# A hybrid block of convolution and attention: the head norm's mean taken out of the value weights once, and values projected without padding columns

## The chip, the cores and the metric

The kernel runs on one core of a Trainium2 chip. The metric is device time in microseconds (us) from a timed execution; the kernel before took 3777.8 us (median of three runs, 3768.41 to 3781.72). The engines of the core are named as in the profile: PE (matrix products), PEld (PE's weight loads, which overlap its products), DVE (vector engine), ACT (scalar engine), POOL (GpSimd) and SP (the engine that issues the transfers here).

## The reference, cut to what matters

The network has six layers on 8 images of 32x32 positions and 128 channels. The change touches the first one only, a retention layer with 8 heads of 16 channels:

```python
vr = (xf @ Wv.T).reshape(B, L, H, HD).transpose(0, 2, 1, 3)
qk = jnp.einsum('bhqd,bhkd->bhqk', qr, kr) * mask[None]
den = jnp.clip(jnp.abs(qk).sum(-1, keepdims=True), 1.0, 50000.0)
qk = qk / den
out = jnp.einsum('bhqk,bhkd->bhqd', qk, vr).transpose(0, 2, 1, 3)
mu = out.mean(-1, keepdims=True)
var = out.var(-1, keepdims=True)
out = (out - mu) / jnp.sqrt(var + LN_EPS) * ln_g + ln_b
out = jax.nn.gelu(out.reshape(B, L, H * HD), approximate=False)
out = out @ Wo.T
```

The mean `mu` runs over the 16 channels of one head. `out` is linear in `vr`, and `vr` is linear in `Wv`, so a head's outputs have mean zero when the 16 rows of `Wv` that belong to the head have their mean subtracted. A convolution layer with an int8-like quantisation follows (the tail of an image below), then gated attention, a mixture of 16 experts, windowed attention, and a graph-routed feed-forward layer; those four are the same instructions before and after.

## The kernel before

The kernel writes out each engine's program by hand; engines meet through semaphores, and the order on each engine is the order of the code. In the retention stage an image is worked through in 32 rounds (4 passes, which are 2 groups of 4 heads times 2 halves of 512 queries, by 8 blocks of 128 keys). A round has the same core for each engine:

- PE: `score` (line 990, 4 products of 512 columns, bf16) for the next round, `norm` (line 1013, 4 f32 products with ones that sum absolute values) of the round before, whatever stands beside the rounds, and `mix` (line 1002, 4 f32 products with the values) of this round.
- DVE: the 4 products of scores with the decay table (line 2120), which free PE's banks and feed `mix`; ACT: 4 absolute values (line 1661), which feed `norm`.

Beside the rounds of image b each engine does the end of image b-1 (`tail`) and the start of image b+1 (`head`). The tuples `PROJECT_AT`, `V_AT`, `MEAN_AT`, `VAR_AT`, `WO_AT` and `CONV_AT` give the rounds in which PE has one such piece: the query and key projections (line 972), the value projections `project_v` (line 978), the head norm's means `row_mean` (line 1019), its variances `row_var` (line 1023), the output projection (line 1028) and the convolution (line 1037). DVE does the partner of such a piece one round later: `center` (line 2039) subtracts the mean that PE spread over the partitions, `rotate` (2027), `tail_add` (2044), `take_sums` (2033 and 2035). ACT squares the centred rows (`square_rows`, 1605) in rounds 7, 15, 23 and 31, takes logarithm and exponential (`invert`, 1590 to 1600) in rounds 2, 10, 18 and 26, and copies projected values out of the accumulation banks (`copy_v`, 1570). POOL divides by the sums (829) and multiplies by the inverse deviation (833).

A head has 16 channels but sits in 32 rows, since `mix` puts 4 heads into 4 strips of 32 partitions. The host lays the value weights out with 16 zero columns behind each head's 16, so `wv` has 256 columns, `project_v` gives 256 columns per block of 128 positions, and `copy_v` writes 512 columns for two blocks, zeros included. `mean_16` averages over the 16 real rows of each strip. Pieces that share bank 7 or bank 6 wait for the reader of the one before (`hn_centered`, `hn_rstd`, `qk_used` and others).

Images 0 and 1 stand apart in PE's program, images 2 to 6 are a loop, image 7 has no head, and an eighth pass of the code has only a tail. The DVE, ACT and POOL programs have a loop over images 1 to 6.

Of the kernel before, what the change touches and what calls it, by code (L numbers as in the profile page):

```python
# [24 lines left out]
P = 128  # L25
# [90 lines left out]
def build(nc, t_in, out_fm):  # L116
    ctx = ExitStack()
    with ctx:
# [83 lines left out]
        wv = sb("wv", [P, HEADS * ROWS])  # L202
# [60 lines left out]
        hn_mean = sem("hn_mean")  # L263
        hn_centered = sem("hn_centered")
# [19 lines left out]
        MEAN_AT, VAR_AT, WO_AT = (13, 21, 29, 5), (17, 25, 1, 9), (7, 15)  # L284
# [519 lines left out]
        def _(pool):  # L804
# [8 lines left out]
            for n, step in enumerate((place_step, pool_step)):  # L813
                pool.memset(pool_spare[:, 2 * n:2 * n + 1], 0.0).then_inc(step, 1)
            pool.memset(zeros16[:], 0.0).then_inc(zero_ready, 2)
# [145 lines left out]
        def _(pe):  # L961
# [13 lines left out]
            def project_v(m, n):  # L975
                for s in range(2):
                    blk = 2 * n + s
                    last = pe.matmul(banks[:, 6 + V_AT[n] % 2, s * 256:(s + 1) * 256], x_head[:, blk * P:(blk + 1) * P], wv[:],
                                     start=True, stop=True)
                last.then_inc(v_proj, 1)  # L980
# [36 lines left out]
            def row_mean(m, p):  # L1017
                pe.wait_ge(o_ready, m * PASSES + (p + 1))
                pe.matmul(banks[:, 7, :], mean_16[:], o_sb[:, p, :], start=True, stop=True).then_inc(hn_mean, 1)

# [20 lines left out]
            def beside(b, r, attend, head, tail, fresh):  # L1041
# [8 lines left out]
                if r in MEAN_AT and (tail if r == MEAN_AT[3] else attend):  # L1050
                    p = MEAN_AT.index(r)
                    if p == 0:
                        pe.wait_ge(hn_rstd, m * (2 * PASSES) + 7) if tail else pe.wait_ge(qk_used, n * 8 + 1)
                    if p == 1:
                        pe.wait_ge(qk_used, n * 8 + 7) if head else pe.wait_ge(hn_rstd, b * (2 * PASSES) + 1)
                    if p == 2:
                        pe.wait_ge(x_mid, m * 2 + 1) if tail else pe.wait_ge(hn_rstd, b * (2 * PASSES) + 3)
                    if p == 3:
                        pe.wait_ge(qk_used, n * 8 + 1) if head else pe.wait_ge(hn_rstd, m * (2 * PASSES) + 5)
                    row_mean(m if p == 3 else b, p)  # L1060
                if r in VAR_AT and (tail if r in VAR_AT[2:] else attend):
                    p = VAR_AT.index(r)
                    if p == 2 and attend:
                        pe.wait_ge(v_ready, b * 4 + 3)
                    if p == 3:
                        pe.wait_ge(wo_added, m * 2 + 1)
                    if p == 0:
                        pe.wait_ge(wo_added, m * 2 + 2) if tail else pe.wait_ge(hn_centered, b * PASSES + 1)
                    if p == 1:
                        pe.wait_ge(gn_head, (n + 1) * 4 + 3) if head else pe.wait_ge(hn_centered, b * PASSES + 2)  # L1070
# [35 lines left out]
                if head and r == 23:  # L1106
                    pe.wait_ge(hn_centered, b * PASSES + 2)
# [4 lines left out]
                if head and r in V_AT[:3]:  # L1112
# [8 lines left out]
                    if i == 2:  # L1121
                        pe.wait_ge(hn_centered, b * PASSES + 3)
# [26 lines left out]
            pe.wait_ge(qk_used, 8)  # L1149
            project_v(0, 0)  # L1150
# [10 lines left out]
            pe.wait_ge(weights_in, 16 * WEIGHT_DMAS)  # L1161
            score(0, 0)
# [398 lines left out]
        def _(act):  # L1561
# [40 lines left out]
            def square_rows(m, p):  # L1602
                act.wait_ge(hn_centered, m * PASSES + (p + 1))
# [322 lines left out]
        def _(dve):  # L1926
# [110 lines left out]
            def center(m, p):  # L2037
                dve.wait_ge(hn_mean, m * PASSES + (p + 1))
# [839 lines left out]
```

## Time and profile before

| what | value |
|---|---|
| timed runs | 3777.8 us median, 3768.41 to 3781.72 |
| profiled execution, span | 3933.9 us (no other time of that execution is given) |
| PE busy over the span | 3090.6 us, 79% |
| DVE busy | 2713.6 us, 69% |
| ACT busy | 1744.7 us, 44% |
| POOL busy | 1548.0 us, 39% |
| retention stage | about the first 1183 us of the span |

The profiled execution is 156.1 us longer than the median of the timed ones. Shares over the whole span mix six layers with different limits; the change lies in the first stage, so that stage is read by itself. In a timeline row the bracket at the end is the time for which the engine had nothing to do before this row, and what ended it; a row without a bracket followed directly on the one before. A row of a window gives its borders and length, then the busy time of each engine in it with the count of instructions, the mean granted clock of PE (1.00 is 2.4 GHz, 0.50 is 1.2 GHz) and the transfers. "x2" counts instructions in the row: an f32 product is recorded as two passes.

### The profile page before, as it was taken

Reading aid. Unit: us, or ns where it says so; the run is one execution under the profiler, and the core shown is the slowest. Engines: PE = TensorE matmul, PEld = TensorE weight load, DVE = VectorE, ACT = ScalarE, POOL = GpSimd, SP = SyncE. Lnnn points to the kernel's source line nnn. Section 1 sums busy time; section 2 is a strip of 40 time slices with the busy share of each in tenths; the row PEclk is TensorE's granted clock in tenths of the full one; section 3 lists DMA queues with packets and bytes.
Section 4 is the critical chain, followed back from the end, with each engine's and each line's share of the span. In section 5 each row is a group of like instructions: output and inputs, shape, how many; then the busy total and the mean of one; then the engine's idle time right before and its main releaser. Section 6 shows DMA issues by size and latency. Waiting matters only on the chain. (4 is left out here: it accounts for less than half of the span.)

```text
span 3933.9 us, 50351 instructions
## 1 busy us (share of the span) xinstructions
PE 3090.6 (79%) x13837; PEld 1485.8 (38%) x13839; DVE 2713.6 (69%) x3835; ACT 1744.7 (44%) x3383; POOL 1548.0 (39%) x1296
## 2 busy tenths in 40 slices
PE   5999999999975763766347777785699999988838
PEld 1222222222211333655225665662255555444412
DVE  4887788778755787999796555661266666666667
ACT  2987887778864562544234444452222222100000
POOL 1121121111000555999862222204366666666500
PEclk9999999999976676999666777776899999999968
DMA  8335415524502213776300111002111111100015
GB/s 268 84 120 152 133 48 147 147 51 129 142 11 71 79 68 120 220 217 207 120 24 27 29 30 29 29 13 51 46 33 31 31 31 25 20 5 5 4 53 203
DMA packets 236635, 319.87 MB, mean 81 GB/s; under 512 B 51789, under 2 KB 172685, under 8 KB 235929
## 3 DMA queue, kind: packets, MB, share of 16 engines
q1 hardware_dynamic: 206744, 296.77, 24.7%
q0 software_dynamic: 29696, 20.97, 3.2%
q8 instruction: 67, 1.10, 0.1%
q14 instruction: 128, 1.04, 0.1%
HBM read 170.95 MB, written 146.67 MB: 81 GB/s over the span
## 5 line engine op out<-in xcount | busy, mean ns | idle before, releaser
L1483 PE MATMUL banks<-arena 128*128 128x512 f32 (+1 forms) x1920 | 741.4, 532 | 56.7 <-DVE arena L2592 50.9
L2592 DVE TENSOR_TENSOR arena<-arena,banks 128x1280 f32<-128x1280 f32 x320 | 468.0, 1486 | 314.4 <-PE banks L1483 216.1
L1483 PEld LDWEIGHTS banks<-arena 128*128 128x128 f32 x1920 | 370.4, 194 | 478.6 <-issue 414.8
L944 POOL DMA_INDIRECT arena<-src_dram,edges_now x336 | 318.3, 947 | 243.9 <-PE banks L1483 119.4
L2120 DVE TENSOR_TENSOR arena<-banks,arena 128x512 f32<-128x512 f32 x512 | 317.7, 683 | 96.1 <-PE banks L990 75.3
L944 POOL DMA_INDIRECT arena<-dst_dram,edges_now x336 | 317.8, 946 | 108.7 <-issue 108.4
L2120 DVE TENSOR_TENSOR keys<-banks,arena 128x512 f32<-128x512 f32 x512 | 317.8, 684 | 60.6 <-PE banks L990 37.7
L2358 DVE TENSOR_TENSOR keys<-keys 128x2048 f32<-128x2048 f32 x132 | 346.1, 2661 | 1.9
L898 POOL TENSOR_TENSOR arena<-arena 128x256 f32<-128x256 f32 x144 | 339.2, 2390 | 19.7 <-ACT arena L1783 19.6
L1661 ACT ACTIVATE arena<-arena 128x512 f32<-128x512 f32 x512 | 288.2, 621 | 129.8 <-DVE arena L2120 89.3
L990 PE MATMUL banks<-arena 96*128 96x512 bf16 x1024 | 281.9, 389 | 35.1 <-DVE arena L2120 32.5
L1661 ACT ACTIVATE keys<-keys 128x512 f32<-128x512 f32 x512 | 281.5, 619 | 53.3 <-PE banks L1013 45.8
L1840 ACT ACTIVATE arena<-arena,mx 128x128 f32<-128x128 f32 x256 | 99.9, 393 | 334.5 <-DVE mx L2416 328.0
L829 POOL TENSOR_TENSOR work<-work,keys 128x512 f32<-128x512 f32 x32 | 40.9, 1279 | 503.4 <-ACT keys L1597 503.4
L808 POOL TENSOR_TENSOR pool_spare<-pool_spare 128x1 f32<-128x1 f32 x54 | 17.8, 329 | 524.3 <-DVE edges_now L2557 241.7
L1303 PE MATMUL banks<-arena 128*128 128x64 bf16 x1152 | 151.3, 307 | 78.0 <-DVE arena L2403 63.7
L990 PEld LDWEIGHTS banks<-arena 96*128 96x128 bf16 x1024 | 80.7, 98 | 339.6 <-DVE arena L2120 119.4
L1886 ACT ACTIVATE arena<-banks,mb 128x512 f32<-128x512 f32 x128 | 87.8, 688 | 241.2 <-PE banks L1468 126.4
L1303 PEld LDWEIGHTS banks<-arena 128*128 128x128 bf16 x1152 | 142.8, 148 | 101.1 <-DVE arena L2403 74.0
L1474 PE MATMUL banks<-arena 128*128 128x512 f32 x256 | 138.2, 630 | 53.7 <-ACT arena L1886 37.5
L1279 PE MATMUL banks<-arena 128*128 128x128 f32 x584 | 104.5, 303 | 94.7 <-POOL arena L898 94.6
L1891 ACT ACTIVATE keys<-banks,mb 128x512 f32<-128x512 f32 x64 | 44.0, 688 | 300.3 <-PE banks L1474 224.2
(397 smaller groups left out, 5727.5 us busy)
## 6 DMA issues: line engine op xcount, KB each, us to landing
sorted_dram<-zeros SPq DMA_DIRECT2D x8, 8192.0 KB, 29.1
arena<-in_w SPq DMA_DIRECT2D x150, 384.0 KB, 4.1
arena<-parts_dram SPq DMA_DIRECT2D x192, 128.0 KB, 4.8
experts_dram<-keys SPq DMA_DIRECT2D x64, 256.0 KB
keys<-experts_dram SPq DMA_DIRECT2D x8, 2048.0 KB, 8.5
parts_dram<-nodes SPq DMA_DIRECT2D x16, 768.0 KB, 3.3
slot_out_dram<-zeros SPq DMA_DIRECT2D x8, 1280.0 KB, 32.0
arena<-sorted_dram SPq DMA_DIRECT2D x150, 64.0 KB, 3.3
```

The lines of the kernel that those rows point to most:

```text
L898: pool.tensor_tensor(slot_hid[:, j % RING], slot_silu[:, j % RING], slot_up[:, j % RING], ALU.mult)\
L944: pool.indirect_dma_start(to[:, s, t, :], None, table[:, :], bass.IndirectOffsetOnAxis(edges_now[:, s, n, t:t + 1].bitcast(U32), 0)).then_ ...
L990: pe.matmul(banks[:, j, :], k_st[0:STACK, head, a * P:(a + 1) * P], q_st[0:STACK, head, halves(qh)], start=True, stop=True).then_inc(score ...
L1279: last = pe.matmul(banks[:, 4 + j % 2, 0:C], slot_hid[:, j % RING, n * P:(n + 1) * P], staged[:, j, 2 * HIDDEN + n * C:2 * HIDDEN + (n + 1 ...
L1303: last = pe.matmul(out, count_low[:, r, :, t], count_high[:, r, :, t], start=start and t == 0, stop=stop and t == CHUNK - 1, skip_group_ch ...
L1474: pe.matmul(banks[:, 6 + i % 2, :], m2[:, e, c, :], mh[:, 2 * (i % 2) + c, :], start=(c == 0), stop=(c == CHUNKS - 1)).then_inc(m_out, 1)
L1483: last = pe.matmul(banks[:, bank, 0:part.shape[1]], ohl[:, s, t, :], part, start=False, stop=False, skip_group_check=True)
L1661: act.activation(a_slots[r % 2][:, j, :], p_slots[r % 2][:, j, :], ACT.Abs).then_inc(absolute, 1)
L1840: act.activation(sc[:, k % 2, j, :], sc[:, k % 2, j, :], ACT.Exp, bias=mx[:, k % 2, 1, j:j + 1], accum_out=mx[:, k % 2, 2, j:j + 1]).then_ ...
L2120: dve.tensor_tensor(p_slots[r % 2][:, j, :], banks[:, j, :], table[:, PER_GROUP * g + j, at:at + HALF], ALU.mult).then_inc(masked, 1)
L2358: dve.tensor_tensor(vo[:, t], vi[:, 0], vi[:, 1], ALU.max if t else ALU.min).then_inc(sort_step, 1)
L2592: dve.tensor_tensor(rh[:, t % RH], oha[:, s, t:t + 1, :].broadcast_to([P, VALS, NB]), vals[:, t, :].unsqueeze(2).broadcast_to([P, VALS, NB ...
```

## The change

The mean is subtracted from the value weights on the chip, once: three small DVE operations after the first image's normalisation (`wv_mean`, a sum over 16 columns per head, a scale, a subtraction), announced by `wv_centered`, for which PE waits before the first `project_v`. `row_mean` and `center` go, and with them 4 PE products and 4 DVE subtractions per image, 32 of each in all. `square_rows` waits for the division (`o_ready`) instead of the subtraction; the PE pieces that waited for `hn_centered` wait for another reader of their bank. `wv` has 128 columns, `project_v` gives 128 columns per block, and `copy_v` reads 256 columns and writes them in groups of 16 with gaps of 16, which POOL has cleared once (`L1["v"]`, announced by `v_cleared`). Instructions of other layers, and the transfers apart from the smaller `wv`, are as they were.

```diff
         wqk = sb("wqk", [P, 4, P])
-        wv = sb("wv", [P, HEADS * ROWS])
+        wv = sb("wv", [P, HEADS * KD])
+        wv_mean = sb("wv_mean", [P, HEADS])
...
-        MEAN_AT, VAR_AT, WO_AT = (13, 21, 29, 5), (17, 25, 1, 9), (7, 15)
+        VAR_AT, WO_AT = (17, 25, 1, 9), (7, 15)
...
+            pool.memset(L1["v"], 0.0).then_inc(v_cleared, 1)
             pool.memset(zeros16[:], 0.0).then_inc(zero_ready, 2)
...
-                    last = pe.matmul(banks[:, 6 + V_AT[n] % 2, s * 256:(s + 1) * 256], x_head[:, blk * P:(blk + 1) * P], wv[:],
+                    last = pe.matmul(banks[:, 6 + V_AT[n] % 2, s * P:(s + 1) * P], x_head[:, blk * P:(blk + 1) * P], wv[:],
...
-            def row_mean(m, p):
-                pe.wait_ge(o_ready, m * PASSES + (p + 1))
-                pe.matmul(banks[:, 7, :], mean_16[:], o_sb[:, p, :], start=True, stop=True).then_inc(hn_mean, 1)
...
-                if r in MEAN_AT and (tail if r == MEAN_AT[3] else attend):
...
-                    row_mean(m if p == 3 else b, p)
...
                     if h == 0:
-                        pe.wait_ge(hn_centered, m * PASSES + 4)
-                    elif attend:
-                        pe.wait_ge(hn_centered, b * PASSES + 1)
+                        pe.wait_ge(qk_used, n * 8 + 1) if head else pe.wait_ge(hn_rstd, m * (2 * PASSES) + 5)
...
+            pe.wait_ge(wv_centered, 1)
             project_v(0, 0)
...
+            pe.wait_ge(v_cleared, 1)
             score(0, 0)
...
-                act.activation(v_sb[:, 2 * n:2 * n + 2, :].rearrange("p k n -> p (k n)"), banks[:, 6 + V_AT[n] % 2, :], ACT.Copy)\
+                if n == 0:
+                    act.wait_ge(v_cleared, 1)
+                act.activation(v_sb[:, 2 * n:2 * n + 2, :].rearrange("p k (h e) -> p (k h) e", h=HEADS)[:, :, 0:KD],
+                               banks[:, 6 + V_AT[n] % 2, 0:2 * P].rearrange("p (k e) -> p k e", e=KD), ACT.Copy)\
                     .then_inc(v_ready, 1)
...
             def square_rows(m, p):
-                act.wait_ge(hn_centered, m * PASSES + (p + 1))
+                act.wait_ge(o_ready, m * PASSES + (p + 1))
...
-            def center(m, p):
-                dve.wait_ge(hn_mean, m * PASSES + (p + 1))
-                dve.tensor_tensor(o_sb[:, p, :], o_sb[:, p, :], banks[:, 7, :], ALU.subtract).then_inc(hn_centered, 1)
...
             head_normalise(0)
+            by_head = wv[:].rearrange("p (h e) -> p h e", h=HEADS)
+            once(dve.tensor_reduce(wv_mean[:], by_head, AX.X, ALU.add))
+            once(dve.tensor_scalar(wv_mean[:], wv_mean[:], 1.0 / KD, None, ALU.mult))
+            dve.tensor_tensor(by_head, by_head, wv_mean[:].unsqueeze(2).broadcast_to([P, HEADS, KD]), ALU.subtract)\
+                .then_inc(wv_centered, 1)
...
-    t["wv"] = head_cols(a["L0_conv_Wv"])
+    t["wv"] = a["L0_conv_Wv"].T
```

On PE in round 5 of image 1, before (990 is `score`, 1013 `norm`, 1019 the mean, 1002 `mix`, 972 a projection):

```order
L990 MATMUL banks<-arena 128x512 [waits masked] x4
L1013 MATMUL banks<-arena,ones 32x512 [waits absolute]
L1013 MATMUL banks<-arena,ones 32x512 x3
L1019 MATMUL banks<-work,mean 128x512 [waits o_ready,qk_used]
L1002 MATMUL banks<-keys,arena 32x512 [waits masked,v_ready]
L1002 MATMUL banks<-keys,arena 32x512 x3
L990 MATMUL banks<-arena 128x512 [waits masked] x4
L1013 MATMUL banks<-keys,ones 32x512 [waits absolute]
L1013 MATMUL banks<-keys,ones 32x512 x3
L972 MATMUL banks<-keys,wqk 128x512 [waits qk_used,head_normed]
```

The same place after, with lines two higher for the same functions:

```order
L992 MATMUL banks<-arena 128x512 [waits masked] x4
L1015 MATMUL banks<-arena,ones 32x512 [waits absolute]
L1015 MATMUL banks<-arena,ones 32x512 x3
L1004 MATMUL banks<-keys,arena 32x512 [waits masked,v_ready]
L1004 MATMUL banks<-keys,arena 32x512 x3
L992 MATMUL banks<-arena 128x512 [waits masked] x4
L1015 MATMUL banks<-keys,ones 32x512 [waits absolute]
L1015 MATMUL banks<-keys,ones 32x512 x3
L974 MATMUL banks<-keys,wqk 128x512 [waits qk_used,head_normed]
```

The mean product between `norm` of round 4 and `mix` of round 5 is gone, and nothing takes its place.

On PE in rounds 28 and 29 of image 1, before (978 is the value projection):

```order
L978 MATMUL banks<-wv,keys 128x256 [waits v_ready]
L978 MATMUL banks<-wv,keys 128x256
L1002 MATMUL banks<-arena 32x512 [waits masked,v_ready]
L1002 MATMUL banks<-arena 32x512 x3
L990 MATMUL banks<-arena 128x512 [waits masked] x4
L1013 MATMUL banks<-arena,ones 32x512 [waits absolute]
L1013 MATMUL banks<-arena,ones 32x512 x3
L1019 MATMUL banks<-work,mean 128x512 [waits o_ready,x_mid]
L1002 MATMUL banks<-keys,arena 32x512 [waits masked,v_ready]
L1002 MATMUL banks<-keys,arena 32x512 x3
L990 MATMUL banks<-arena 128x512 [waits masked] x4
L1013 MATMUL banks<-keys,ones 32x512 [waits absolute]
```

The same place after:

```order
L980 MATMUL banks<-wv,keys 128x128 [waits v_ready]
L980 MATMUL banks<-wv,keys 128x128
L1004 MATMUL banks<-arena 32x512 [waits masked,v_ready]
L1004 MATMUL banks<-arena 32x512 x3
L992 MATMUL banks<-arena 128x512 [waits masked] x4
L1015 MATMUL banks<-arena,ones 32x512 [waits absolute]
L1015 MATMUL banks<-arena,ones 32x512 x3
L1004 MATMUL banks<-keys,arena 32x512 [waits masked,v_ready]
L1004 MATMUL banks<-keys,arena 32x512 x3
L992 MATMUL banks<-arena 128x512 [waits masked] x4
```

The value projection keeps its two products with half the columns, and the mean of round 29 is gone.

## Rows read from the trace of the kernel before

**Rows 1.** Two images: busy (count) of PE, PEld, DVE, ACT, POOL; clock; DMA.

```profile
187.50:323.50 136.00, 127.64 (x722) 32.41 (x721) 110.30 (x188) 110.52 (x181) 24.03 (x16) 0.99 0.42 118
463.40:603.20 139.80, 132.29 (x723) 32.78 (x722) 110.39 (x189) 110.86 (x182) 23.66 (x16) 0.95 0.41 115
```

**Rows 2.** Groups by line: shapes, count, busy us, mean ns, idle before.

```profile
L1019 PE MATMUL banks<-work,mean 128*128 128x512 f32 x64 | 36.9, 660 | 5.1 <-POOL work L829 5.1
...
L2039 DVE TENSOR_TENSOR work<-work,banks 128x512 f32<-128x512 f32 x32 | 22.0, 686 | 11.6 <-PE banks L1019 11.6
...
L1570 ACT ACTIVATE arena<-banks 128x512 f32<-128x512 f32 x32 | 18.5, 579 | 2.2 <-PE banks L978 2.2
...
L1782 ACT ACTIVATE arena<-banks 128x256 f32<-128x256 f32 x144 | 55.6, 386 | 58.8 <-PE banks L1271 45.6 <-POOL arena L898 12.7
```

**Rows 3.** Timeline of PE, round 5: start, length, name, idle before.

```profile
619.79 1.13 PE L1019 MATMUL banks<-work,mean 128*128 128x512 f32 x2
620.85 1.06 PE L1002 MATMUL banks<-keys,arena 128*32 128x512 f32 x8
```

**Rows 4.** Timeline of DVE, the subtraction after that product.

```profile
620.96 0.69 DVE L2039 TENSOR_TENSOR work<-work,banks 128x512 f32<-128x512 f32 x1 [0.21 <-PE banks L1019]
622.27 2.48 DVE L2120 TENSOR_TENSOR keys<-banks,arena 128x512 f32<-128x512 f32 x4 [0.63 <-PE banks L990]
```

**Rows 5.** Timeline of PE, round 21 and the start of round 22.

```profile
546.50 1.12 PE L1019 MATMUL banks<-work,mean 128*128 128x512 f32 x2
...
550.34 0.39 PE L990 MATMUL banks<-arena 96*128 96x512 bf16 x1 [1.72 <-DVE arena L2120]
```

**Rows 6.** Timeline of DVE, after round 15 and in round 22.

```profile
523.42 0.69 DVE L2044 TENSOR_TENSOR work<-work,banks 128x512 f32<-128x512 f32 x1 [1.07 <-PE banks L1028]
...
549.60 2.48 DVE L2120 TENSOR_TENSOR arena<-banks,arena 128x512 f32<-128x512 f32 x4
```

**Rows 7.** Timeline of PE, the wait of round 12 in two images.

```profile
231.97 1.07 PE L1013 MATMUL banks<-keys,ones 128*32 128x512 f32 x8 [2.21 <-ACT keys L1661]
...
507.88 1.93 PE L1013 MATMUL banks<-keys,ones 128*32 128x512 f32 x8 [2.21 <-ACT keys L1661]
```

**Rows 8.** Timeline of PE, rounds 26 and 28 of one image.

```profile
568.90 0.39 PE L990 MATMUL banks<-arena 96*128 96x512 bf16 x1 [2.09 <-DVE arena L2120]
...
573.10 2.08 PE L978 MATMUL banks<-wv,keys 128*128 128x256 f32 x4
...
583.61 1.13 PE L978 MATMUL banks<-wv,keys 128*128 128x256 f32 x4
584.67 1.07 PE L1002 MATMUL banks<-arena 128*32 128x512 f32 x8
```

**Rows 9.** Timeline of PE, 128-column f32 products of a later stage.

```profile
1703.08 1.06 PE L1271 MATMUL banks<-arena 128*128 128x128 f32 x8
1703.97 0.27 PE L1264 MATMUL banks<-ident,arena 128*128 128x128 f32 x1
```

**Rows 10.** Timelines of DVE and of PE's weight loads, where two images meet.

```profile
597.04 2.48 DVE L2120 TENSOR_TENSOR arena<-banks,arena 128x512 f32<-128x512 f32 x4 [2.45 <-issue]
...
599.58 0.10 PEld L990 LDWEIGHTS banks<-arena 96*128 96x128 bf16 x1 [0.50 <-DVE arena L2120]
```

**Rows 11.** Timelines of ACT and PE after the last image's last round.

```profile
1146.12 0.81 ACT L1609 ACTIVATE work<-work,lngb 128x512 f32<-128x512 f32 x1 [0.78 <-POOL work L833]
...
1147.84 2.08 PE L1028 MATMUL banks<-work,wo 128*128 128x512 f32 x2 [0.78 <-DVE work L2039]
```

**Rows 12.** Timeline of ACT, round 23 of the first image.

```profile
155.36 2.19 ACT L1661 ACTIVATE keys<-keys 128x512 f32<-128x512 f32 x4 [0.39 <-PE banks L1013]
```

**Rows 13.** Timelines of DVE and POOL at the start of the program.

```profile
19.47 0.69 DVE L2027 TENSOR_TENSOR keys<-banks,arena 128x512 f32<-128x512 f32 x1 [2.17 <-PE banks L972]
...
0.94 0.53 POOL L815 MEMSET zeros<- 128x512 bf16 x1
23.16 1.26 POOL L819 TENSOR_TENSOR keys<-keys 128x512 f32<-128x512 f32 x1 [21.70 <-DVE keys L2027]
```

More of the change, by code:

```diff
@@ L262, in build @@
         sum_step = sem("sum_step")
-        hn_mean = sem("hn_mean")
-        hn_centered = sem("hn_centered")
+        wv_centered = sem("wv_centered")
+        v_cleared = sem("v_cleared")
         hn_var = sem("hn_var")
@@ L1049, in beside @@
                     project_v(b, 3)
-                if r in MEAN_AT and (tail if r == MEAN_AT[3] else attend):
[L1051 to L1059, printed above, removed]
-                    row_mean(m if p == 3 else b, p)
                 if r in VAR_AT and (tail if r in VAR_AT[2:] else attend):
                     p = VAR_AT.index(r)
-                    if p == 2 and attend:
-                        pe.wait_ge(v_ready, b * 4 + 3)
+                    if p == 2:
+                        pe.wait_ge(v_ready, b * 4 + 3) if attend else pe.wait_ge(x_mid, m * 2 - 1)
                     if p == 3:
@@ L1067, in beside @@
                     if p == 0:
-                        pe.wait_ge(wo_added, m * 2 + 2) if tail else pe.wait_ge(hn_centered, b * PASSES + 1)
+                        pe.wait_ge(wo_added, m * 2 + 2) if tail else pe.wait_ge(qk_used, n * 8 + 1)
                     if p == 1:
-                        pe.wait_ge(gn_head, (n + 1) * 4 + 3) if head else pe.wait_ge(hn_centered, b * PASSES + 2)
+                        pe.wait_ge(gn_head, (n + 1) * 4 + 3) if head else pe.wait_ge(hn_rstd, b * (2 * PASSES) + 1)
                     row_var(m if p >= 2 else b, p)
@@ L1106, in beside @@
                 if head and r == 23:
-                    pe.wait_ge(hn_centered, b * PASSES + 2)
+                    pe.wait_ge(qk_used, n * 8 + 7)
                     head_mean(n + 1)
@@ L1121, in beside @@
                     if i == 2:
-                        pe.wait_ge(hn_centered, b * PASSES + 3)
+                        pe.wait_ge(x_mid, m * 2 + 1) if tail else pe.wait_ge(hn_rstd, b * (2 * PASSES) + 3)
                     project_v(n, i)
@@ L2059, in beside @@
                     rotate(n, PROJECT_AT.index(r - 1))
-                if r - 1 in MEAN_AT:
-                    p = MEAN_AT.index(r - 1)
-                    if p == 3 and tail:
-                        center(m, 3)
-                    elif p < 3 and attend:
-                        center(b, p)
                 if tail and r - 1 in WO_AT:
@@ L2816, in lay_out @@
     t["edges"] = a["L3_ffn_edge_index"].reshape(2, P, COLS)
-    def head_cols(w):
-        full = np.zeros((C, HEADS, ROWS), w.dtype)
-        full[:, :, :KD] = w.T.reshape(C, HEADS, KD)
-        return full.reshape(C, HEADS * ROWS)
     swap = np.arange(C) ^ 1
     t["wqk"] = np.stack([a["L0_conv_Wq"].T, a["L0_conv_Wq"][swap].T, a["L0_conv_Wk"].T, a["L0_conv_Wk"][swap].T], 1)
-    t["wv"] = head_cols(a["L0_conv_Wv"])
+    t["wv"] = a["L0_conv_Wv"].T
     wo = np.zeros((HEADS, ROWS, C), np.float32)
```

## The prediction

> **What bounds the kernel now.** I read the page's slices first, then the windows of single images in the retention stage, then the timelines of PE, DVE and ACT through one image, stopping wherever PE's row has a bracket. The windows say which engine fills an image: in the steady one PE is busy for 132.3 of 139.8 us, DVE for 110.4 and ACT for 110.9 [rows 1]. So PE bounds the stage, but not all the time: 7.5 us of the image PE stands still. The timeline shows where. One wait is in round 12 (2.21 us, for ACT's absolute values) [rows 7], one in round 22 (1.72 us, for DVE's table products) [rows 5], one in round 26 (2.09 us, DVE again) [rows 8]; the rest is in short ones beside these. Everywhere else PE's rows follow each other without a bracket, and DVE has brackets that name PE [rows 4]. Whatever PE loses in such a full stretch, the image loses; what it loses ahead of one of the waits only lengthens the wait.
>
> A second thing to see is the clock. The same wait of 2.21 us is followed by 8 passes that take 1.07 us in image 1 and 1.93 us in the steady image [rows 7], which is 2.4 against 1.2 GHz; the mean granted clock is 0.99 there and 0.95 here, and the image takes 136.0 against 139.8 us [rows 1]. The work is the same, so 3.8 us of the steady image are the clock's.
>
> **The mean products.** 64 passes make 32 products [rows 2]. In a full stretch one costs from its own start to the start of what follows, 620.85 - 619.79 = 1.06 us [rows 3]; the 660 ns mean of a pass counts the overlap twice. An image has four, in rounds 5, 13, 21 and 29. Those of rounds 5, 13 and 29 stand in full stretches: 3 x 1.06 = 3.2 us per image. The one in round 21 does not. There DVE goes from 523.42, where it last waited for PE, through its statistics and the normalisation of the image before to the table product at 549.60 [rows 6], and PE, whose mean product starts at 546.50, waits 1.72 us for that [rows 5]. Without the product PE waits 2.8 us. I take nothing for it; the bound on the other side is 1.06.
>
> **The subtractions on DVE.** 32 of 0.686 us [rows 2]. Between two table products DVE waits 0.21 us for PE, subtracts for 0.69 and waits for PE another 0.63 [rows 4], 1.53 us together. Take PE's 1.06 away, and 0.47 us of waiting for PE is left: DVE stays the one that waits, which is also why the whole 1.06 is taken as gained above. None lies in DVE's chain to the waits of rounds 22 and 26. Worth 0, at most 0.7 each. The squares on ACT no longer wait for them, which matters only at the end of the stage.
>
> **The value projection.** In a full stretch a `project_v` costs 584.67 - 583.61 = 1.06 us for 4 passes of 256 columns [rows 8]. For 128 columns the nearest row is a later stage's: 8 passes begin at 1703.08 and the next product at 1703.97, so 0.11 us a pass, 0.45 for four [rows 9]. Saved: 0.6 us; the bounds are 0 (the weight loads, which stay, set the pace) and 0.7 (a third of the time left). The Trainium skill, "TensorE: Matmul & The Clock Gate", section "LDWEIGHTS (loading the stationary operand)", speaks against a full halving: a weight load takes its number of columns over 1.2, in ns, so 107 ns for 128, and here the image's block is the weight, unchanged. By that, four passes cannot take under 0.43 us as an estimate, a saving of 0.63; the trace's 0.11 us a pass agrees.
>
> Of the four in an image, that of round 0 and that of round 28 are in full stretches: 2 x 0.6. That of round 26 runs at the lower clock, 2.08 us [rows 8]; half of it is 1.0. That of round 31 is lost: DVE comes over its loop's end with 2.45 us in which it waits for nothing, and PE's next `score` is released by its table product (0.50 us) [rows 10]. So 2.2 us per image.
>
> `copy_v` goes from 579 ns towards the 386 of a 128x256 copy [rows 2], 32 times 0.2 us on ACT, in stretches where ACT waits for PE: 0. That its write has gaps no row shows; were it as slow as now, nothing changes, and at double, 0.6 us each, ACT's waits still cover it.
>
> **Images of another shape.** Image 0 has no tail and thus not the two DVE waits, but ACT is nearly the limit: in round 23 it waits just 0.39 us for PE [rows 12]. I give it 1.06 (round 13), 0.4 (round 21), 0.9 (round 29) and 0.8 for two value projections: 3.2. Images 1 to 6 get 3.2 + 2.2 = 5.4 each, 32.4. Image 7 gets three means and one projection: 3.8. In the last tail nothing lies beside the chain. `Gelu` on ACT begins at 1146.12 for 0.81 us, and PE's output projection at 1147.84, because of the mean and the subtraction [rows 11]; without them it follows the `Gelu` at 1146.97, 0.9 us sooner. At the start value projections stand once alone in a chain of PE and ACT: at the lower clock one is shorter by 1.0 and its two copies by 0.2 each, if no transfer is later; so 0 to 1.4, and I take 0.7.
>
> **What is added.** Three DVE operations on 128x128 or less fit into the 2.17 us for which DVE waits before its first rotation [rows 13]; the nearest row, 0.69 us for 512 columns, makes them 2.1 us at most. The clearing of 2048 f32 columns on POOL: 512 of bf16 took 0.53, so four to eight times that, 2 to 4 us, and POOL has nothing before 23.16 [rows 13]. Both 0. No wait is new in a loop: the pieces of PE that waited for the subtraction now wait for rotations or deviations that are rounds old.
>
> Sum: 3.2 + 32.4 + 3.8 + 0.9 + 0.7 = 41.0 us. The profiled execution's 3933.9 would become 3893; it is 156.1 us above the median of the timed runs, and since nothing shows where these lie I subtract the same 41 from 3777.8: 3737 us.
>
> **The rivals.** (1) The clock comes back. If a wait no longer drops the clock, as in image 1, each of images 2 to 6 gains up to 3.8 us more, 19 in all: 3718. For it: the same pause did not drop it in image 1. Against: images 2 to 6 are one loop, and the steady one has it. The mirror of it, a longer half-rate stretch in some places, is in the range too.
>
> (2) The round becomes bound elsewhere. If a round without its mean product is held by ACT or DVE, as in round 21 and in image 0, the products of rounds 5, 13 and 29 are worth a third or nothing and the projections remain: 7 x 2.2 + some 4, 20 us: 3758. Against: the 0.47 us for which DVE would still wait for PE in such a round [rows 4]; ACT has 29 us of idle time per image [rows 1].
>
> (3) Slower. PE's wait in round 22 grows from 1.7 to 2.8 us, and the clock stays low from there to the wait of round 26. Between these, from 550.3 to 566.8 (568.90 less its wait), PE is the bound for 16.5 us [rows 5, 8]. A mean clock of 0.95 means a tenth of the image, 14 us, at half rate [rows 1], some 5 us behind each of the three waits. If all 16.5 were at half rate the other 11.5 would take as long again: 11.5 - 5.4 = 6.1 us more per image in six images, less the 8.6 us saved in images 0 and 7 and at both ends: +28, 3806 us. It decides once the low clock costs 5.4 us more per image than now. For it: a value projection 4 us behind the wait of round 26 was still at 2.08 us [rows 8]. Against: the mean clock of 0.95 leaves no room for more than such short stretches after any of the pauses as they are [rows 1]. The same page of the Trainium skill, section "HAM oscillation — how this bites in real kernels", says that a pause of the engine can throttle it again, so that the burst behind starts cold; of the two images in [rows 7] one agrees and one does not.
>
> (4) The change does nothing measurable: the profiled execution has waits that the timed ones have not, or the other way round. 3778.
>
> **How the numbers follow.** Forecast 0.62, (1) 0.17, (2) 0.12, (3) 0.05, (4) 0.04. The time is the forecast's, 3737. The measurement tells about 0.3% from no change, 11 us. The range reaches to rival (1) and a little past, and up past (2), since the runs before spread over 13 us: 3712 to 3764. Faster by over 0.3% are the forecast, (1) and nearly all of (2): 0.90; within 0.3% 0.06; slower 0.04.
>
> **What would show it.** In the profile after: image windows of about 134.4 us in place of 139.8, PE busy about 125 us; PE's wait in round 22 at 2.8 us and those in rounds 12 and 26 as they are; value projections of four passes that take 0.45 to 0.5 us to the next start; the wait at the images' boundary longer by 0.6 on PE; the later layers as long as before. Images that stay near 139 with new brackets on PE in rounds 5 to 8 would mean rival (2), a mean granted clock above 0.97 or below 0.92 in the steady images (1) or (3).

## The result, and the profile after

The changed kernel takes 3772.3 us (median of 12 runs, 3764.0 to 3782.9) against 3781.1 us for the kernel before (12 runs, 3768.4 to 3793.4). The medians lie 8.7 us apart. The ratio on record is 0.9964, with a 95% interval of 0.9952 to 0.9976; it is not the quotient of the two medians (0.9977), and by it the gain is some 14 us. Either way the gain is measurable and small. The forecast was 3737 us, a gain of 41, in a range of 3712 to 3764.

First the windows of the retention's images, one row an image, in the order length, busy time and count of PE, PEld, DVE, ACT and POOL, granted clock, DMA share and GB/s. Here are images 1 and 2 and one of the later ones, of the changed kernel.

```profile
183.34:319.76 136.42, 127.42 (x714) 31.63 (x713) 107.77 (x185) 109.85 (x181) 23.66 (x16) 0.94 0.42 118
319.76:456.02 136.26, 123.55 (x707) 31.08 (x709) 108.01 (x184) 109.75 (x181) 23.66 (x16) 0.95 0.45 124
456.02:596.33 140.31, 127.78 (x717) 31.92 (x721) 108.03 (x183) 109.60 (x181) 23.68 (x16) 0.93 0.39 115
```

PE's busy time has fallen by 4.5 us in the later images, as was to be expected of the instructions taken out, and yet such an image takes 140.3 us where it took 139.8 [rows 1]. Image 1 takes 136.4 where it took 136.0, at a clock of 0.94 where it had 0.99. So PE stands still for longer, 12.5 us instead of 7.5, and what it does runs slower.

The timeline of PE shows two places. The first is where the loop's body ends and begins again (round 31 of one image and round 0 of the next):

```profile
726.57 0.71 PE L980 MATMUL banks<-wv,keys 128*128 128x128 f32 x4
727.21 1.06 PE L1004 MATMUL banks<-keys,arena 128*32 128x512 f32 x8
730.71 1.03 PE L992 MATMUL banks<-arena 96*128 96x512 bf16 x4 [2.43 <-issue]
731.67 1.47 PE L1015 MATMUL banks<-keys,ones 128*32 128x512 f32 x8
733.07 0.58 PE L980 MATMUL banks<-wv,keys 128*128 128x128 f32 x1
735.70 0.80 PE L980 MATMUL banks<-wv,keys 128*128 128x128 f32 x3 [2.05 <-issue]
736.43 1.94 PE L1004 MATMUL banks<-arena 128*32 128x512 f32 x8
738.30 1.38 PE L992 MATMUL banks<-arena 96*128 96x512 bf16 x4
```

Two brackets of 2.43 and 2.05 us have `issue` as their releaser: no other engine is waited for. That PE's own instructions were not there is a reading of them, which the next rows and the experiments test. Even a value projection is cut in two, one pass and then three. Behind them 8 passes take 1.94 us, the lower clock. Each of the loop's four turns back has such a pair of brackets, 17.9 us in all (10.0 on `score`, 7.9 on the projection). The kernel before has no such bracket inside its retention loop. The branch at the loop's end tells the same: duration in ns, minimum, median and maximum, of the kernel before and then of the changed one.

```profile
L1165 PEldq COMPARE_BRANCH  x5: 83/215/232, 455.9 to 1014.0; - x5
```

```profile
L1152 PEldq COMPARE_BRANCH  x5: 83/4828/5084, 444.3 to 1007.2; - x5
```

The queue that brings instructions agrees: packets, MB and share, of the whole page, before and after. From 600 to 760 us it moves 10 packets in the changed kernel; from 460 to 620 us of the kernel before it has none. Over the whole loop, from 330 to 1000 us, the queue moves 41 packets in the changed kernel and 6 in the kernel before, these 6 ahead of 460 us.

```profile
q8 instruction: 67, 1.10, 0.1%
```

```profile
q8 instruction: 84, 1.38, 0.2%
```

The second place is round 22, which answers to [rows 5]:

```profile
677.71 1.04 PE L1004 MATMUL banks<-keys,arena 128*32 128x512 f32 x8
681.66 2.40 PE L992 MATMUL banks<-arena 96*128 96x512 bf16 x4 [2.91 <-DVE arena L2100]
683.99 1.93 PE L1015 MATMUL banks<-keys,ones 128*32 128x512 f32 x8
685.86 0.37 PE L1090 MATMUL banks<-ident,small 128*1 128x128 f32 x1
686.15 1.87 PE L1004 MATMUL banks<-arena 128*32 128x512 f32 x8
```

The wait has grown from 1.72 to 2.91 us, and the products behind it run at the lower clock for longer. In the same place the kernel before had this:

```profile
552.61 1.94 PE L1013 MATMUL banks<-keys,ones 128*32 128x512 f32 x8
554.47 0.37 PE L1105 MATMUL banks<-ident,small 128*1 128x128 f32 x1
554.77 1.48 PE L1002 MATMUL banks<-arena 128*32 128x512 f32 x8
```

So the first 8 passes behind the wait were at half rate already. The change lengthens that stretch: the second 8 now take 1.87 us, and the four `score` products 2.40. A value projection in a full stretch takes 727.21 - 726.57 = 0.64 us where it took 1.06 [rows 8], more than the 0.45 to 0.5 that was forecast. In the last tail PE's output projection follows `Gelu` directly (1135.30 - 1134.34 = 0.96 us, where it was 1.72 [rows 11]). Of ACT, then of PE:

```profile
1134.34 0.81 ACT L1599 ACTIVATE work<-work,lngb 128x512 f32<-128x512 f32 x1 [0.77 <-POOL work L835]
```

```profile
1135.30 3.49 PE L1026 MATMUL banks<-work,wo 128*128 128x512 f32 x4 [7.16 <-ACT work L1599]
```

The layers behind the retention play no part. In the changed kernel's execution they take 2605 us (the span less the last convolution product's start, as in the table below), and in eleven of the experiments' twelve 2591 to 2605. In the twelfth they take 2612 us, and in the profiled execution of the kernel before 2752. The excess of 156 us of that execution thus lies in them and not in its retention: 1181.8 us, which a run with the same retention repeats (1184.7).

### The profile page after: what moved, and what is told of

Same layout as the page of the kernel before. It is cut to its first block and busy times, and to the rows that moved or that the text cites. A ratio compares the mean times of both kernels' runs of the same rounds, so it can differ in the third digit from the quotient of the medians.

```text
span 3772.9 us, 50157 instructions
## 1 busy us (share of the span) xinstructions
PE 3018.5 (80%) x13775; PEld 1464.9 (39%) x13775; DVE 2700.6 (72%) x3806; ACT 1732.5 (46%) x3383; POOL 1547.7 (41%) x1297
## 3 DMA queue, kind: packets, MB, share of 16 engines
q8 instruction: 84, 1.38, 0.2%
## 5 line engine op out<-in xcount | busy, mean ns | idle before, releaser
L1470 PE MATMUL banks<-arena 128*128 128x512 f32 (+1 forms) x1920 | 725.7, 524 | 13.3 <-DVE arena L2577 13.1
L992 PE MATMUL banks<-arena 96*128 96x512 bf16 x1024 | 291.9, 400 | 51.2 <-DVE arena L2100 38.2
L913 POOL DMA_INDIRECT arena<-slot_out_dram,arena x128 | 158.5, 1238 | 43.8 <-issue 43.6
```

Source lines behind the costliest of these rows:

```text
L913: pool.indirect_dma_start(made[:, j, :], None, slot_out_dram[:, :], bass.IndirectOffsetOnAxis(rows_now[:, j:j + 1].bitcast(U32), 0)).then_ ...
L992: pe.matmul(banks[:, j, :], k_st[0:STACK, head, a * P:(a + 1) * P], q_st[0:STACK, head, halves(qh)], start=True, stop=True).then_inc(score ...
L1470: last = pe.matmul(banks[:, bank, 0:part.shape[1]], ohl[:, s, t, :], part, start=False, stop=False, skip_group_check=True)
```

## The experiments

Two theories stood against each other and a third beside them. **Fetch:** the loop's body is shorter and stands elsewhere in PE's program, and there it no longer stays in PE's instruction memory. **Clock:** idle time that the change adds ahead of PE's half-rate stretches lowers the granted clock. **Waits:** the image is held by ACT and DVE, rival (2) of the prediction. The table holds all runs. "Retention" is the start of its last convolution product in the profiled execution; "images" are the windows of images 1 to 5, and beside them their granted clocks; ratio and interval are against the kernel before as it was timed with each. The experiments were timed in three groups: both loops placed, loop misplaced, attention loop moved and mean's part; retention loop placed, V's part, products in round 13 and in round 21; and the last four. Across groups the ratios compare better than the medians.

| kernel | median us | ratio, 95% interval | retention | images | clock in them |
|---|---|---|---|---|---|
| before | 3781 to 3787 | 1 | 1181.8 | 136.1 to 140.1 | 0.95 to 0.99 |
| after | 3772.3 | 0.9964 [0.9952, 0.9976] | 1167.6 | 136.3 to 141.5 | 0.92 to 0.95 |
| after, both loops placed | 3748.8 | 0.9899 [0.9877, 0.9920] | 1152.2 | 133.9 to 136.5 | 0.94, 0.95 |
| after, retention loop placed | 3754.4 | 0.9908 [0.9883, 0.9932] | 1150.7 | 132.0 to 136.5 | 0.94 to 0.97 |
| before, retention loop misplaced | 3839.5 | 1.0142 [1.0119, 1.0164] | 1233.0 | 138.4 to 148.7 | 0.93 to 0.96 |
| before, attention loop moved | 3789.4 | 1.0008 [0.9991, 1.0025] | 1184.7 | 137.7 to 140.0 | 0.95 to 0.98 |
| placed, mean's part alone | 3753.9 | 0.9914 [0.9897, 0.9931] | 1154.4 | 131.7 to 137.6 | 0.94 to 0.99 |
| before, V's part alone | 3765.9 | 0.9950 [0.9933, 0.9966] | 1161.1 | 134.7 to 138.5 | 0.95 to 0.99 |
| placed, product in round 13 | 3745.6 | 0.9893 [0.9869, 0.9917] | 1149.9 | 134.5 to 136.3 | 0.95, 0.96 |
| placed, product in round 21 | 3738.2 | 0.9871 [0.9848, 0.9893] | 1131.7 | 129.3 to 133.3 | 0.96 to 1.00 |
| placed, product in round 22 | 3765.4 | 0.9952 [0.9935, 0.9969] | 1158.7 | 134.8 to 136.6 | 0.94, 0.95 |
| placed, products in 21 and 11 | 3742.3 | 0.9893 [0.9872, 0.9913] | 1133.6 | 129.5 to 133.2 | 0.96 to 1.00 |
| placed, products in 21, 11, 25 | 3735.7 | 0.9860 [0.9835, 0.9884] | 1131.7 | 129.5 to 134.7 | 0.95 to 1.00 |
| before, products in 11 and 25 | 3767.4 | 0.9952 [0.9934, 0.9970] | 1160.5 | 134.4 to 136.0 | 0.99, 1.00 |

**The changed kernel with both loops placed.** The body of the retention's loop begins at PE's instruction 3009 of the compiled program before (counted without labels, 1655 long) and at 2976 in the changed one (1635 long). Waits on a semaphore that has long reached its value move it; two of them make one instruction.

```
+            for _ in range(66):                       # ahead of head_mean(0)
+                pe.wait_ge(consts_in, 16 * CONST_DMAS)
...
+            for _ in range(446):                      # behind the retention
+                pe.wait_ge(consts_in, 16 * CONST_DMAS)
```

> The changed kernel, with satisfied waits added to TensorE's program at two places where it is idle: 33 instructions ahead of the first head mean, which put the body of the retention loop back at the place (modulo 256 instructions) where it stands in the kernel before, and 223 between the retention and the windowed attention, which keep the attention's loop body where the changed kernel has it (modulo 256). Theory (instruction fetch): in the changed kernel the retention loop no longer stays in TensorE's instruction memory, so each backward branch waits for its instructions (2.4 and 2.0 us at the first two rounds, a branch of 4.8 to 5.1 us, and a low clock behind it). Here these waits go (branch 0.1 to 0.3 us, no instruction fetches inside the loop), the images of the loop fall from 140.3 to about 136 us, the stage ends some 18 us earlier (about 1150 us), and the kernel takes 3750 to 3760 us. Rival A (the images are bound by what ScalarE and VectorE hand over): the waits for instructions go but the images stay at 140 us, time as the changed kernel, 3772. Rival B (the clock falls because TensorE has less to do): images stay at 140 us at a granted clock of 0.93 or less.

3748.8 us, just under the 3750 to 3760 of the fetch theory. The branch is at 0.21 us (median), and the queue moves 6 packets from 330 to 1000 us. An image of the loop:

```profile
453.64:588.49 134.85, 125.80 (x714) 31.40 (x713) 107.81 (x185) 109.64 (x181) 23.66 (x16) 0.95 0.43 119
```

At the kernel before's clock, 0.95, it takes 134.85 us, 4.95 less than before. If ACT and DVE held the image, as the waits theory has it, it would not have become shorter.

**The kernel before with its retention loop misplaced.** The same waits, 446 ahead of `head_mean(0)` and 66 behind the retention, in the kernel before.

> The kernel before with nothing changed but its place: 223 satisfied waits ahead of the first head mean, so that the retention loop's body begins at the place (modulo 256 instructions) that it has in the changed kernel, and 33 behind the retention, so that everything after it stands as in the kernel before. Fetch theory: the retention loop now fetches its instructions in every turn; each image of the loop goes from 139.8 to 144 to 145 us, the kernel from 3781 to about 3800 us. Rivals A and B: no fetch matters, 3781 within 5.

It went the theory's way, but by 57 us instead of 20. Of that, 22.6 us are the waits themselves, which here the whole start stood behind; DVE's first normalisation begins at 39.08 us and not at 16.49.

```profile
39.08 0.81 DVE L2017 TENSOR_SCALAR keys<-keys,small 128x1024 f32<-128x1024 f32 x1
```

The retention ends 51.2 us later, less 22.6 is 28.6 us. Of these, 2.8 stand in images 0 and 1, ahead of the loop, where its fetches cannot reach; the other 26 are what a misplaced loop costs, with nothing else changed. From 330 to 1000 us the queue moves 40 packets. The branch and an image of the loop:

```profile
L1167 PEldq COMPARE_BRANCH  x5: 83/4871/5298, 479.8 to 1067.0; - x5
```

```profile
491.84:638.20 146.36, 133.72 (x725) 32.96 (x729) 110.67 (x187) 110.78 (x181) 23.67 (x16) 0.94 0.40 110
```

**The kernel before with its attention loop moved.** 358 waits between the retention and the attention, which bring the attention's loop to where the changed kernel has it.

> The kernel before with 179 satisfied waits of TensorE between the retention and the windowed attention alone, so that the attention loop's body begins where it begins in the changed kernel (modulo 256 instructions). Fetch theory: no fetches within the attention loop, its stage falls from 681 us to about 660 us as in the changed kernel, and the time from 3781 to about 3760 us, with none of the change in it. Rivals: stage and time as in the kernel before, within 5 us.

This missed. No time was gained (1.0008), although the instruction fetches within that loop did go: in its stage the queue moves 10 packets, and 28 in the kernel before. Its stage, from the first product with `wqkv` on V's side to the last transposition, takes 662 us in this run, and 649 in the run before this one, whose loop fetches throughout. The 682 us from which I had taken a gain of 20 belong to the one execution that was profiled. In this stage, where PE often waits for DVE and ACT, the fetches cost nothing that the times show.

**The change in halves.** First the mean's part with V padded as before, both loops placed as in the first run.

```
+        wv = sb("wv", [P, HEADS * ROWS])
...
+            by_head = wv[:].rearrange("p (h e) -> p h e", h=HEADS)[:, :, 0:KD]
```

> The changed kernel with V projected with its zero padding as before (the mean's part alone), with the same added waits as the first run of this call, both loops placed alike. By the prediction's terms the narrower projection is 2.2 us an image (0.6 in rounds 0 and 28, 1.0 in round 26), so this should be some 15 us slower than the first run (about 3770). If the narrower projection hides behind other work, it is as fast as the first run.

3753.9, 5 us behind the first run and not 15: nearer the second reading. Then V's part in the kernel before, its mean products kept.

```
...
-                    last = pe.matmul(banks[:, 6 + V_AT[n] % 2, s * 256:(s + 1) * 256], x_head[:, blk * P:(blk + 1) * P], wv[:],
+                    last = pe.matmul(banks[:, 6 + V_AT[n] % 2, s * P:(s + 1) * P], x_head[:, blk * P:(blk + 1) * P], wv[:],
...
```

> The kernel before with V projected without its zero padding and nothing else changed (its retention loop stands one instruction later, which the fetch theory calls harmless). The prediction's terms: 0.6 us each in rounds 0 and 28, 1.0 in round 26, 15 us in all (3766). By the run of the mean's part alone, which was only 5 us behind the run of both, 2 to 6 us (3777).

3765.9, a ratio of 0.995: 19 us, above the 15 of the terms and far above 2 to 6. Alone the parts shorten the retention by 20.7 us (V) and 27.4 us (mean), together by 31.1 (retention loop placed), not 48. An image of each tells why, the mean's part first (two images of one execution), V's second:

```profile
458.24:589.96 131.72, 122.83 (x714) 31.17 (x713) 107.81 (x185) 110.42 (x181) 23.66 (x16) 0.99 0.44 122
589.96:727.53 137.57, 128.90 (x714) 32.13 (x713) 107.80 (x185) 110.65 (x181) 23.64 (x16) 0.94 0.42 117
```

```profile
598.90:733.80 134.90, 126.22 (x722) 31.56 (x721) 110.31 (x189) 109.84 (x181) 24.04 (x16) 0.99 0.43 119
```

The same instructions take 131.7 us at a clock of 0.99 and 137.6 at 0.94. In the run of V's part the clock rises from 0.95 in image 1 to 0.99 in images 4 and 5, in that of the mean's it reaches 0.99 in one image alone. The durations add, the clock does not.

**The retention's loop placed and nothing more.** The first run without its second group of waits.

> The changed kernel with the 33 added instructions ahead of the first head mean alone; the 223 behind the retention are left out, so the attention's loop stands elsewhere. By the runs so far the place of the attention's loop is worth nothing (660 us with and without fetches), so this should be as fast as the run with both pads or a few us faster: 3742 to 3750 us. If the attention's place does matter, 3760 to 3770.

3754.4 (3744 to 3758), above the 3742 to 3750 expected and not apart from the first run. The branch is back at a fifth of a microsecond, and this is the kernel from which the next runs are built. One image at each of two clocks:

```profile
L1154 PEldq COMPARE_BRANCH  x5: 76/208/227, 449.8 to 989.1; - x5
```

```profile
457.30:593.60 136.30, 127.37 (x714) 31.66 (x713) 107.77 (x184) 109.71 (x181) 23.64 (x16) 0.94 0.42 118
593.60:725.70 132.10, 123.02 (x715) 30.80 (x713) 107.87 (x185) 109.69 (x181) 23.66 (x16) 0.97 0.43 122
```

**One mean product put back.** Its result is unused and nothing is subtracted; the retention's loop stays at 3009. In round 13 first:

```
+                if r == 13 and attend:
+                    pe.wait_ge(hn_rstd, m * (2 * PASSES) + 7) if tail else pe.wait_ge(qk_used, n * 8 + 1)
+                    pe.wait_ge(o_ready, b * PASSES + 1)
+                    pe.matmul(banks[:, 7, :], mean_16[:], o_sb[:, 0, :], start=True, stop=True)
```

> The run before this one (changed kernel, retention loop at the old place) with the averaging product of round 13 back on TensorE, its result unused and nothing subtracted. The prediction's theory: round 13 is no wait's cover, so the product costs its full 1.06 us an image, 8 us in all, and if the half-rate stretches fall on it somewhat more. Rival (the images are bound by ScalarE or VectorE): nothing. Second rival (a product that TensorE computes keeps its clock up): nothing or a gain, at a granted clock of 0.95 instead of 0.94.

It was to cost 8 us and cost nothing: 3745.6 against 3754.4, with intervals that overlap, at a clock of 0.95 and 0.96 in place of 0.94 to 0.97. So more work in a full stretch came with a slightly higher clock too; whether it raised it, one run does not tell. The same in round 21:

> The same with the averaging product of round 21 back instead, its result unused. The prediction's theory: the wait of round 22 on VectorE's table product shrinks from 2.9 to 1.8 us and the time stays, within 2 us of the kernel without it; that is what made this one of the four products free. Rival: it costs 1.06 us an image like the other, 8 us. Second rival (clock): less idle time ahead of the half-rate stretch, a gain of some us.

3738.2 against 3754.4: more work, 16 us less time, the clock theory's side (14 by the ratios). Two images, and PE's rounds 21 and 22:

```profile
187.80:317.10 129.30, 121.05 (x716) 30.79 (x715) 107.74 (x185) 109.42 (x181) 23.64 (x16) 1.00 0.43 125
448.60:581.70 133.10, 125.57 (x716) 31.46 (x715) 107.66 (x184) 109.50 (x181) 23.65 (x16) 0.96 0.42 121
```

```profile
528.87 1.13 PE L1051 MATMUL banks<-work,mean 128*128 128x512 f32 x2
529.93 1.07 PE L1004 MATMUL banks<-keys,arena 128*32 128x512 f32 x8
532.71 0.39 PE L992 MATMUL banks<-arena 96*128 96x512 bf16 x1 [1.71 <-DVE arena L2105]
...
534.82 1.07 PE L1015 MATMUL banks<-keys,ones 128*32 128x512 f32 x8
```

The wait is 1.71 us again, and the 8 passes behind it take 1.07 us, not 1.94. The windows of images 0 to 5 give the clock's share: their lengths times what is missing of the clock to 1.00 add up to 36 us with the retention loop placed and nothing more, and to 17 with the product in round 21. The difference, 19 us, accounts for all by which the retention became shorter (1150.7 to 1131.7, of which 1.1 us is an earlier start, since fewer waits are added there). The control is the same product issued one round later, behind that wait (`if r == 22 and attend:`).

> As the run with the unused product in round 21 (3738 us), but the product is issued one round later, behind the wait of round 22 instead of ahead of it. The work is the same, the idle time of round 22 is not filled. Clock theory (idle time of TensorE ahead of the stretches from 84 and 102 us into an image is what drops the clock): the wait stays at 2.9 us, an image has 13.7 to 17.1 us at half rate as without the product, and the time is 3750 to 3760. Rival (it is the work added, not where it stands, or the product's other effects): 3738 as with the product in round 21.

```profile
535.90 1.04 PE L1004 MATMUL banks<-keys,arena 128*32 128x512 f32 x8
539.85 2.40 PE L992 MATMUL banks<-arena 96*128 96x512 bf16 x4 [2.91 <-DVE arena L2105]
542.18 1.94 PE L1015 MATMUL banks<-keys,ones 128*32 128x512 f32 x8
544.05 2.08 PE L1051 MATMUL banks<-work,mean 128*128 128x512 f32 x2
```

3765.4: 27 us slower by the medians and 31 by the ratios than with the product ahead of the wait, at the same count of instructions and the same loop position. Where the product stands decides. Behind the wait it fills no idle time and runs at half rate itself, 2.08 us in seven of the eight images and 1.06 in the first, 16 us in all; this run is 11 us slower than the one without any product by the medians, and 17 by the ratios (0.9952 against 0.9908).

**Filling the other waits.** An unused product in round 11, ahead of the wait of round 12, and then one in round 25 as well, ahead of the wait of round 26:

```
+                if r == 11 and head and attend:
+                    pe.wait_ge(qk_used, n * 8 + 4)
+                    pe.matmul(banks[:, 6, :], wqk[:, 0, :], x_head[:, halves(0)], start=True, stop=True)
+                if r == 25 and head and attend:
+                    pe.wait_ge(gn_head, (n + 1) * 4 + 3)
+                    pe.matmul(banks[:, 7, :], wqk[:, 0, :], x_head[:, halves(0)], start=True, stop=True)
```

> The kernel with the unused product in round 21 (3738 us), and one more unused product of 1.06 us in round 11, ahead of the wait of 2.2 us of round 12. Clock theory: the wait falls to 1.1 us, the half-rate stretch at 43 us into an image (3.4 us in two images of five) goes, and the time is the same or up to 5 us shorter: 3732 to 3738. Rival (a product costs its duration): 8 us longer.

> As the run before, and a third unused product in round 25, ahead of the wait of 2.1 us of round 26 (it stands ahead of the variance product of round 25, so it delays that by 1 us). Clock theory: the half-rate stretch from 100 us into an image goes as well, images of 129 to 130 us at a granted clock of 0.99 to 1.00, and 3720 to 3732 us. Rival: each product costs its 1.06 us an image, 16 us longer than with the one of round 21 alone (3754).

The one in round 11 did not pay: 3742.3 (3737 to 3751) beside 3738.2 (3725 to 3740). Its images take 129.5 to 133.2 us as without it, and its retention ends 1.9 us later; but the ratios, 0.9893 and 0.9871, are 8 us apart with overlapping intervals, so the rival's cost of 8 us is not excluded. With all three it is 3735.7, not apart from the product in round 21 alone; I had hoped for 3720 to 3732. Some images have the full clock and some do not:

```profile
317.20:446.70 129.50, 123.23 (x721) 31.33 (x719) 107.72 (x184) 109.46 (x181) 23.70 (x16) 1.00 0.45 125
446.70:581.40 134.70, 129.04 (x721) 32.12 (x719) 107.79 (x184) 109.65 (x181) 23.67 (x16) 0.95 0.42 119
```

Last, the two products in the kernel before, with nothing taken out and no other edit (its loop begins 16 instructions later and still stays):

> The kernel before with two unused products of 1.06 us added, in round 11 and in round 25, ahead of the waits of rounds 12 and 26, and nothing taken out. Clock theory: images of 139.8 us with 13.7 us at half rate become some 136 us (as image 1 of the kernel before, 136.1 with 3.4 us at half rate): 15 to 25 us faster, 3760. Rival (a product costs its duration): 16 us slower, 3800.

```profile
459.50:593.90 134.40, 128.16 (x726) 32.46 (x725) 110.31 (x188) 110.45 (x181) 24.03 (x16) 1.00 0.43 120
```

3767.4, a ratio of 0.9952: two useless products bring the kernel before as much as the whole change did when it was made. Here too the clock accounts for it: what is missing of it to 1.00, times the lengths of images 0 to 5, falls from 29 to 8 us, and the retention is 21.3 us shorter.

## Why the prediction was wrong, point by point

**The terms of the sum held in all, not one by one.** Image 0 was to gain 3.2 us and gained 3.1 (115.8 to 112.7); a steady image 5.4, and at an equal clock of 0.95, with the loop in its place, the loop's three images at that clock, in two runs, gained 4.95 to 5.5; the last tail 0.9, measured 0.8. A value projection was to gain 0.6 in a full stretch, measured 1.06 - 0.64 = 0.42: a pass of 128 columns took 0.16 us here and not the 0.11 of [rows 9]. By halves, at an equal clock of 0.99 [rows 1], the mean's part gives 136.0 - 131.7 = 4.3 where 3.2 was forecast, and V's 136.0 - 134.9 = 1.1 where 2.2 was. The clock is given to 0.01, which is about 1 us of an image, so the two sizes are rough. Their sum, 5.4, is the forecast's; as far as the halves were mis-sized, that they cancel is luck. The wait of round 22 was forecast at 2.8 us and is 2.91; those of rounds 12 and 26 are as they were. Rival (2) is out.

**"No wait is new in a loop" failed.** It looked at the waits that the code writes. PE's wait for its own instructions is written nowhere; it came from the loop's body beginning 33 instructions earlier. That the body is also 20 instructions shorter did no harm: 1635 of them at 3009 do not stall, and 1655 at 3232 do. It cost 21 us of time (0.9964 to 0.9908 of some 3781, over two jobs) and 16.9 us in the retention (1167.6 to 1150.7). In the kernel before, the same misplacement costs some 26. The Trainium skill, "Runtime: NRT & Kernel Launch", section "Instruction fetch mechanics", says that a taken branch to an instruction outside the window held makes the engine wait for a fetch; the branches of 4.8 us agree. It also says that such a window is two pages and that there is no instruction cache; it gives TensorE more memory than that, 2048 instructions, without saying which of the two its window is. With two pages the body of 1655 instructions would stall wherever it stands. Here the measurement decides otherwise: it branches back in 0.2 us, with no packet on the queue from 460 to 1000 us, at one place, and stalls at another.

**"The one in round 21 ... I take nothing for it" failed in its sign.** The bounds were 0 and a gain of 1.06 us. Below 0 there was room that I excluded without a row: the product filled idle time, and without it the stretch at half rate behind the wait is longer. With the loop in its place, taking it out costs 16 us (3738.2 to 3754.4). This is the mirror that rival (1) mentioned and the mechanism of rival (3), in small. Image 1, which had 0.99, shows it most: in the changed kernel it gains nothing (136.4 us), with the loop placed 1.9 to 2.2 us, with round 21 filled 6.8. But the wait of round 22 is not the only thing that decides. In the run of V's part, image 1 keeps the product of round 21 and a wait of 1.71 us, and has a clock of 0.95 all the same; and with the loop placed, images with the same wait of 2.9 us differ between 0.94 and 0.97. What decides between such images is open.

**Together.** The retention was to become 41 us shorter. Placed and with round 21 filled, it is 50.1 us shorter (1181.8 to 1131.7), for then the clock comes back on top, as rival (1) had it. Emptying round 21 takes 19.0 us of that away, and the misplaced loop another 16.9; 14.2 us are left, which is the result. Seen from the forecast: with the loop placed the retention is 31.1 us shorter, 9.9 short of 41. By the windows' clocks of images 0 to 5 the lower clock took 29 us before and takes 36 there, which is 7 of them, and the waits that place the loop delay the start by 2 (DVE's first normalisation at 18.58 us in place of 16.49). The chances were wrong in that the one loss had no place among the rivals and the other only one at its extreme, with 0.05.

## What to carry to other kernels

Count idle time ahead of a busy stretch of TensorE as something that can cost more than itself: with one product of 1.06 us ahead of a wait the images of this stage take 129.3 to 133.3 us at a granted clock of 0.96 to 1.00, without it 132.0 to 136.5 at 0.94 to 0.97. Before work is removed ahead of a wait, look at the granted clock behind that wait. Where stretches at half rate follow it, take from the full stretches first, and time the kernel once with the filler left in. After any change in a long loop, look for `issue` brackets and long branches at its back edge, since placement alone was worth 21 us here, more than the change brought as it was made.

## What the runs showed of the hardware that was not expected

- A loop of 1655 instructions on TensorE ran without fetches when it began at instruction 3009 (6 packets on the instruction queue from 330 to 1000 us, all ahead of 460 us) and fetched in every turn when it began at 3232, which is 256 less 33 further on (40 packets). The changed kernel's, of 1635, fetched at 2976 (41 packets) and did not at 3009 (6). Both places at which they fetched are the same modulo 256. The packets on the queue are 16.4 KB each (1.38 MB in 84). Which places are good in general these runs do not tell.
- The same fetches in the attention's loop cost nothing measurable (1.0008, interval 0.9991 to 1.0025).
- Satisfied waits are not free where an engine is waited for: 223 instructions of them delayed the start by 22.6 us, 0.1 us each.
- An unused product of 1.06 us, ahead of a wait, made the kernel 16 us faster; behind the same wait, 11 us slower than without it by the medians (3765.4 against 3754.4) and 17 by the ratios. How much of a wait has to be filled is open: with three filled, images still differ between clocks of 0.95 and 1.00.
- The fastest of the kernels, with the loop placed and round 21 filled, alone or with the two other products, take 3738 and 3736 us, 0.987 and 0.986 of the kernel before. The forecast's time can be reached, but not by the change alone.
